# Unread bf16 products streamed through TensorE at four places of a two-layer audio tower

## The chip, the cores and the metric

The kernel runs on one core of a Trainium2 chip. The metric is the device time of one launch in microseconds (us), smaller is better. The core's engines work side by side and meet at semaphores: TensorE (PE, matrix products and transposes into the eight PSUM banks), VectorE (DVE), ScalarE (ACT), GpSimd (POOL, no access to PSUM) and SyncE (SP, which only issues DMAs here). The hardware profiler also records which clock was granted to TensorE: 1.00 in a row is 2.4 GHz, 0.50 is 1.2 GHz.

## What is computed

Sixteen signals of 4096 samples become 16 x 255 tokens of 64 values, and two layers follow, each attention plus a mixture of experts. Cut to what matters:

```python
h = tok(x)                      # interpolate 4x, windows of 64, |fft|, soft minimum: (16, 255, 64)
h = h + attn0(layernorm(h))     # 8 heads, rank 32 scores, softmax over 255 tokens, 64x64 value-output matrix per head
h = h + moe0(layernorm(h))      # 16 experts 64 -> 128 -> 64, relu, top 2; plus own residual and layernorm with gain
h = h + attn1(layernorm(h))     # 8 heads of 8, softmax of content scores blended with a softmax of positions
h = h + moe1(layernorm(h))      # 8 experts 64 -> 64 -> 64, gelu, top 2
```

Everything is fp32 (a few operands are split into bf16 parts that add up to fp32 precision).

## The kernel before

Tokens lie in SBUF as 32 tiles of 128 rows x 64 values (`res`), two tiles per signal; a chunk is 4 tiles, so there are 8 chunks (`CH`, `TC`). The program has two phases with a barrier between them. The phase `tokens` makes the tokens and ends on DVE and ACT, with nothing for PE after its last transform. The phase `experts0_to_experts1` holds both layers as two blocks, `attention0_and_experts0` and `attention1_and_experts1`. In each block every engine has one program, written out by hand with loops over pairs of signals in the middle of the attentions; the order of work on an engine is the order of the text, and semaphores say when a step may start. Engines run from one stage straight into the next, and the stretches where one stage drains and the next fills are called joins here.

**Start of attention 0.** DVE makes averages, variances and the first normed tiles. PE's `x_columns(c)` transposes chunk c into bank 5 or 6 (L695, four 128x128 transposes), ACT or DVE copies it out, POOL makes the normed tiles of chunks 2 to 7 (L1328). `project` makes queries and keys (L708) or values (L712) into banks 7 and 4, ACT copies them (L930), `scores` (L720) writes banks 0 to 3, and DVE takes the maxima (L1152). DVE's `inverse_roots(1, ...)`, for which POOL's L1328 waits, stands behind the first maxima in DVE's order.

**Attention 0 to experts 0.** After the last signal PE runs `outputs_turn` and `weights(0)` (L630, transposes of the routing weights of chunk 0, which DVE makes: L1055, L1057), then `duos`: per chunk and pair of experts `hidden` (L644), ReLU on ACT (L904), `second` (L655), weighting on DVE (L1138, L1097).

**First join, experts 0 to attention 1.** PE turns the positional weights of the eight heads (`pos_turn`, L1671, banks 2 and 3, copied out by ACT in `pos_out`, L1952), turns the chunks of the new input (`x_columns` of this block, that is `ColumnParts.turn`, L404, banks 0, 1, 5), and turns the last sum of the experts (`e0.sum_turn`, L663). ACT, DVE and POOL split each turned chunk into bf16 parts (L409, L413, L419, L420, L424), the last chunks only after the last normalisation of the experts (DVE L1078 to L1089, POOL L465 to L469, ACT L880 and L886). `values(c)` (L1684) and `pos_values(n)` (L1700) use the parts and the turned weights; after that the attention loop starts.

**Second join, attention 1 to experts 1.** `x_turn` (L1784), `logits` (L1797), and the tail of the attention (`slot` with "tail": L1651, L1591, L1597) alternate on PE, while DVE reads the logits and picks experts (`best`, L2215 to L2222), and makes the routing weights of the first four chunks (`combine(0)`, L2233 to L2252). PE's `weights(0)` and `weights(1)` (L1803) wait for these. Then per chunk c and group g: `hidden` (L1817), gelu on ACT (L2048), `spread` (L1829, routing weights to all rows, banks 4 and 5), `weigh` on DVE (L2269), `second` (L1839, L1842), and per chunk `sum_turn` (L1852), with `x_turn` and `logits` of chunks 6 and 7 among the first two chunks. `w64`, which the change reads, holds bf16 weights, written in the phase `tokens` and only read afterwards.

Of the kernel before, what the change touches and what calls it, by code (L numbers as in the profile page):

```python
# [25 lines left out]
P = 128  # L26
B, SIG = 16, 4096
# [16 lines left out]
H = 8  # L44
# [43 lines left out]
def tower(nc, x, taps, consts, w_raw, gate_b0, w1_01, b1_0, w2_0, b2_0, gamma,  # L88
          split_sel, wpos, wproj, bproj, b1_1, w2_1, b2_1, out):
    with ExitStack() as ctx:  # L90
# [4 lines left out]
        ps = ctx.enter_context(nc.psum_tensor("ps", [P, 8, 512], F32))  # L95
# [12 lines left out]
        w64 = sb("w64", [P, 3, W64 - W32], BF16)  # L108
# [43 lines left out]
        def sem(name):  # L152
            held.append(nc.alloc_semaphore(name))
            return held[-1]
# [8 lines left out]

        def chain(eng, name):
            return Chain(eng, sem(name))

# [323 lines left out]
        def attention0_and_experts0(block, later):  # L492
            QUADS = 2
# [45 lines left out]
            def columns_copied(eng, c):  # L539
                if c < BY_ACT:  # L540
                    eng.wait_ge(s_col_a, c + 1)
                else:
                    eng.wait_ge(s_col_d, c - BY_ACT + 1)
# [59 lines left out]
            def _(pe):  # L603
# [83 lines left out]
                def x_columns(c):  # L687
                    if c < 2:
                        pe.wait_ge(s_x, c + 1)
                    else:  # L690
                        pe.wait_ge(s_xp, c - 1)
                    if c >= 2:
                        columns_copied(pe, c - 2)
                    for k in range(TC):
                        last = nc.tensor.transpose(ps[:, COLUMN_BANK[c % 2], P * k:P * k + P], x2[:, TC * c + k].rearrange("p a d -> p (a d)"), ident)  # L695
                    last.then_inc(s_turned, 1)
# [18 lines left out]
                def scores(k):  # L715
                    par, g = at(k)
                    for tq in range(2):
                        for i in range(4):
                            r = slice(32 * i, 32 * i + 32)
                            last = nc.tensor.matmul(S[:, i, tq], qk[par][r, g, 0, P * tq:P * tq + P], qk[par][r, g, 1], start=True, stop=True)  # L720
                    last.then_inc(s_S, 1)
# [22 lines left out]
                def outputs_turn(par):  # L744
                    for tq in range(2):
                        last = nc.tensor.matmul(OT[:, tq], o_sb[par][:, P * tq:P * tq + P], fold[:], start=True, stop=True)
                    last.then_inc(s_OT, 1)
# [18 lines left out]
                def slot(j, k, more=True, route=None):  # L766
# [41 lines left out]
                        route()  # L808
                    second_turn(k, N, 1)

                x_columns(0)
                x_columns(1)
                columns_copied(pe, 0)
                project(QKN, 0, 0, 0)
                pe.wait_ge(s_out, 2)
                scores(0)
                project(VN, 0, 1, 0)
                x_columns(2)
                x_columns(3)
# [20 lines left out]
                pe.wait_ge(s_O, B)  # L840
                pe.wait_ge(s_add, B - 1)
                outputs_turn((B - 1) % 2)
                weights(0)

                duos(0, 0)
# [601 lines left out]
        def attention1_and_experts1(block, e0):  # L1447
            scale = (D // H) ** -0.5
            QUADS = 2
# [97 lines left out]
            def _(pe):  # L1547
# [163 lines left out]
                pos_turn(1)  # L1711
                x_columns(1)
                pos_turn(2)
                x_columns(2)
                pos_turn(3)
                e0.sum_turn()
                for h in range(4, H):
                    pos_turn(h)
                x_columns(3)
                x_columns(4)  # L1720
                values(0)
                x_columns(5)
                values(1)
                x_columns(6)
                values(2)
                x_columns(7)
                values(3)
                project(0, 0)
                pos_values(0)
                pos_values(1)  # L1730
                values(4)
# [130 lines left out]
                x_turn(3)  # L1862
                logits(2)
                x_turn(4)
                slot(B // 2, 6, ("tail",))
                logits(3)
                x_turn(5)
                slot(B // 2, 7, ("tail",))
                logits(4)
                logits(5)  # L1870
                hidden(0, 0)
                pe.wait_ge(s_O, QUADS * B)
                for d in range(2):
                    weights(d)
                for c in range(CH):
                    hidden(c, 1)
                    if c == 0:
                        pe.wait_ge(s_fin, B)
                        for d in range(2, 4):
                            weights(d)  # L1880
                    spread(c, 0)
                    if c >= 1:
                        second(c - 1, 1)
                    if c < 2:
                        x_turn(6 + c)
                    if c == 3:
                        pe.wait_ge(s_wgt, GROUPS * c + 1)
                        for d in range(4, CH):
                            weights(d)
                    if c < CH - 1:  # L1890
                        hidden(c + 1, 0)
                    if c < 2:
                        logits(6 + c)
                    spread(c, 1)
                    if c >= 1:
                        sum_turn(c - 1)
                    if c == 0:
                        pe.wait_ge(s_ct, 4)
                    second(c, 0)
# [626 lines left out]
```

## Time and profile before

| | us |
|---|---|
| median of 3 runs | 752.44 (750.17 to 752.70) |
| profiled execution | 751.62 |
| span of its trace | 749.8 |
| PE busy | 649.9 (87%) |
| DVE busy | 570.5 (76%) |
| ACT busy | 503.1 (67%) |
| POOL busy | 334.4 (45%) |
| mean granted TensorE clock | 0.937 |

The busy times overlap. The end of a matmul is modelled and matmuls are pipelined, so a busy PE isn't PE at its peak. The chain that ended last is 55% PE, 23% DVE and 8% issue by share of the span. In the chain each piece is what the end of the execution waited for at that moment; a piece of PE there can be shorter than the same work in the timeline, since the next piece starts before its modelled end. The clock of 0.937 is an average over long stretches at 1.00 and some at 0.50.

### The profile page before, as it was taken

The numbers are of one execution on the slowest core, as the hardware profiler recorded it, in microseconds if no ns is written. First come the engines' busy times: TensorE is split into PE (matmuls) and PEld (weight loads), VectorE is DVE, ScalarE is ACT, GpSimd is POOL, SyncE is SP. The second block draws the span as 40 slices with busy tenths as digits, with TensorE's granted clock in tenths as the row PEclk, the third lists the DMA queues.
The fourth block names the chain that finished last, engine by engine and source line by source line (L and its number), as shares of the span: only waits on it lengthen the run. The fifth ranks groups of instructions, "written<-read, shape, count | busy, mean of one in ns | idle before, by whom it ended". The sixth has DMA issues, their size and how long they took to land.

```text
span 749.8 us, 16418 instructions
## 1 busy us (share of the span) xinstructions
PE 649.9 (87%) x4984; PEld 357.5 (48%) x4984; DVE 570.5 (76%) x1647; ACT 503.1 (67%) x1264; POOL 334.4 (45%) x417
## 2 busy tenths in 40 slices
PE   5528998999999988999999996799898888779896
PEld 5514665666666653333232225455555555453332
DVE  6675787777777776899999978589888888773653
ACT  3646877888888863567777767477777777624542
POOL 1006678788787866133333325624554545300000
PEclk9857999999999999999999998799999999965998
DMA  4030000000000002523323330000000000000001
GB/s 109 1 112 1 1 2 1 0 0 0 0 0 0 1 1 85 200 102 108 104 98 96 99 109 1 2 2 1 1 0 0 0 0 0 2 0 2 15 19 24
DMA packets 22038, 24.37 MB, mean 33 GB/s; under 512 B 12390, under 2 KB 12902, under 8 KB 21734
## 3 DMA queue, kind: packets, MB, share of 16 engines
q1 hardware_dynamic: 19751, 23.31, 9.9%
q10 hardware_dynamic: 2239, 0.49, 0.3%
q8 instruction: 22, 0.36, 0.2%
q14 instruction: 26, 0.21, 0.1%
HBM read 22.48 MB, written 1.31 MB: 32 GB/s over the span
## 4 chain that ended last, share of the span: by engine, by line
PE 55%; DVE 23%; issue 8%; ACT 3%; POOL 2%; DMA 2%; DVEq 0%; SPq 0%; ACTq 0%; POOLq 0%
PE ps L726 8%; PE ps L762 7%; PE ps L1563 5%; DVE big L1097 4%; PE ps L1585 4%; PE ps L720 4%; DVE big L1138 3%; DVE big L2077 3%; PE ps L1839 2%; PE ps L1569 2%; PE ps L1817 2%; PE ps L644 2%; PE ps L708 2%; PE ps L712 2%; DVE big L1055 2%
## 5 line engine op out<-in xcount | busy, mean ns | idle before, releaser
L1344 POOL TENSOR_TENSOR big<-big 128x1024 f32<-128x1024 f32 x64 | 119.8, 1893 | 45.7 <-DVE big L1158 45.7
L942 ACT ACTIVATE big<-ps,big 128x255 f32<-128x255 f32 x256 | 117.0, 483 | 12.2 <-DVE big L1152 9.7
L904 ACT ACTIVATE big<-ps,b1s 128x512 f32<-128x512 f32 x128 | 80.2, 678 | 32.5 <-PE ps L644 31.1
L1152 DVE TENSOR_REDUCE big<-ps 128x4 f32<-128x1020 f32 x64 | 75.1, 1212 | 26.7 <-PE ps L720 26.7
L1935 ACT ACTIVATE big<-ps 128x1024 f32<-128x1024 f32 x64 | 65.9, 1030 | 33.0 <-PE ps L1575 30.6
L2077 DVE TENSOR_REDUCE big<-ps 128x4 f32<-128x1020 f32 x64 | 78.0, 1219 | 6.9 <-DVE res L2134 2.5
L726 PE MATMUL ps<-cst,big 128*128 128x128 f32 x512 | 76.7, 283 | 6.3 <-POOL big L1344 2.4
L1164 DVE COPY mid<-ps 128x512 f32<-128x512 f32 x96 | 63.4, 685 | 18.3 <-PE ps L726 15.1
L726 PEld LDWEIGHTS ps<-cst,big 128*128 128x128 f32 x512 | 54.2, 140 | 40.8 <-issue 21.5
L644 PE MATMUL ps<-big,wall 64*128 64x512 f32 x256 | 72.8, 645 | 0.7 <-ACT big L875 0.7
L655 PE MATMUL ps<-big,w2s 128*64 128x512 f32 x256 | 69.9, 625 | 2.1 <-ACT big L904 1.2
L762 PE MATMUL ps<-mid,big 128*64 128x256 f32 (+1 forms) x512 | 69.5, 392 | 0.0
L1138 DVE SCALAR_TENSOR_TENSOR big<-ps,b2s,mid 128x512 f32<-128x512 f32 x64 | 47.9, 749 | 18.6 <-issue 8.8
L942 ACT ACTIVATION_READ_ACCUMULATOR big<-ps,big 128x1 f32 x256 | 55.6, 217 | 0.0
L465 POOL TENSOR_TENSOR big<-big 128x4 f32<-128x4 f32 x16 | 16.2, 1015 | 86.1 <-DVE big L455 85.6
L1563 PE MATMUL ps<-big,selqk 128*128 128x256 bf16 x384 | 52.8, 273 | 0.7 <-ACT big L1911 0.4
L1097 DVE TENSOR_TENSOR big<-big 128x512 f32<-128x512 f32 x56 | 44.2, 790 | 0.0
L930 ACT ACTIVATE big<-ps 128x512 f32<-128x512 f32 x64 | 34.9, 600 | 10.8 <-PE ps L708 9.8
L460 POOL TENSOR_TENSOR mid<-mid 128x2 f32<-128x2 f32 x16 | 11.5, 717 | 66.4 <-DVE mid L455 66.4
L1563 PEld LDWEIGHTS ps<-big,selqk 128*128 128x128 bf16 x384 | 32.7, 97 | 17.2 <-issue 13.5
L1569 PE MATMUL ps<-big 64*128 64x256 bf16 x256 | 25.4, 273 | 17.8 <-DVE big L2077 17.6
L720 PE MATMUL ps<-big 32*128 32x256 f32 x512 | 37.6, 408 | 2.9 <-ACT big L942 1.7
(274 smaller groups left out, 1327.9 us busy)
## 6 DMA issues: line engine op xcount, KB each, us to landing
mid<-spread_w SPq DMA_DIRECT2D x128, 128.0 KB, 2.8
mid<-in_split_sel SPq DMA_DIRECT2D x1, 1536.0 KB, 7.4
wall<-in_w SPq DMA_DIRECT2D x1, 1280.0 KB, 6.4
out_tokens<-res SPq DMA_DIRECT2D x16, 56.0 KB, 1.6
cst<-in_consts SPq DMA_DIRECT2D x1, 520.5 KB, 5.0
pexp<-in_w_raw SPq DMA_DIRECT2D x1, 512.0 KB, 6.3
w2s<-in_w SPq DMA_DIRECT2D x1, 512.0 KB, 3.3
mid<-in_taps ACTq DMA_DIRECT2D x1, 320.0 KB, 3.9
```

Source lines behind the costliest of these rows:

```text
L644: last = nc.tensor.matmul(H1(e, j), wst[0][half, f:f + P], xc[q][half], start=True, stop=True)
L655: last = nc.tensor.matmul(Y(e)[D * j:D * j + D], w2s[0][:, 2 * e + j], hid[e % 2][j], start=True, stop=True)
L726: last = nc.tensor.transpose(AT[:, j, c, P * tq:P * tq + P], e_sb[r % 4][:, j, tq, P * c:P * c + P], ident)
L762: last = nc.tensor.matmul(O[D * j:D * j + D, par], val[par][0:n, c, D * h:D * h + D], a_sb[r % 4][0:n, j, c], start=(g == 0 and a == 0 and ...
L904: last = nc.scalar.activation(hid[e % 2][j], H1(e, j), ACT.Relu, bias=b1s[0][:, 2 * e + j:2 * e + j + 1])
L942: last = nc.scalar.activation(e_sb[r % 4][:, jj, tq, 0:NW], S[:, 2 * (r % 2) + jj, tq, 0:NW], ACT.Exp, scale=-1.0, bias=minus[r % 4][:, jj ...
L1097: ins = nc.vector.tensor_tensor(acc[q], acc[q], part[e % 2], ALU.add)
L1138: nc.vector.scalar_tensor_tensor(out=acc[q] if e == 0 else part[e % 2], in0=Y(e), scalar=b2s[:, e:e + 1], in1=cb[e % RING], op0=ALU.add, o ...
L1152: nc.vector.tensor_reduce(minus[r % 4], S[:, 2 * a:2 * a + 2, :, 0:NW], AX.X, ALU.min).then_inc(s_mx, 1)
L1344: nc.gpsimd.tensor_tensor(e_sb[r % 4], e_sb[r % 4], bc(inverse[r % 4].unsqueeze(3), [P, 2, 2, 256]), ALU.mult).then_inc(s_A, 1)
L1563: last = nc.tensor.matmul(out_, selqk[:, 2 * p + n, part], parts[par][:, part], start=(part == 0), stop=(part == 2))
L2077: nc.vector.tensor_reduce(mx[k % 2], S[:, :, :, 0:NW], AX.X, ALU.max).then_inc(s_max, 1)
```

## The change

A helper `stream(bank, n)` issues n products of 128x128 by 128x512 in bf16 from `w64` into one PSUM bank; nothing waits for them, nothing reads them, and what they leave in the bank is overwritten by the next real product. It is called ahead of and among the first columns of attention 0 (14, 2, 3, 5 and 3 products), ahead of the first routing weights of experts 0 (5), in the first join (6, 3, 6, 2, 4, 3 and 6) and in the second (6, 6, 9 and 3): 86 products. Where a bank is still being read, the wait that the next user of the bank has anyway is repeated or moved ahead of the stream. No other instruction changes.

```diff
--- before.py
+++ after.py
@@ -163,6 +163,12 @@
 
         def chain(eng, name):
             return Chain(eng, sem(name))
+
+        def stream(bank, n):
+
+            weights = w64[:].rearrange("p n f -> p (n f)")
+            for _ in range(n):
+                nc.tensor.matmul(ps[:, bank], weights[:, 0:P], weights[:, 0:512], start=True, stop=True)
 
 
 
@@ -808,12 +814,17 @@
                         route()
                     second_turn(k, N, 1)
 
+                stream(0, 14)
                 x_columns(0)
+                stream(0, 2)
                 x_columns(1)
+                stream(0, 3)
                 columns_copied(pe, 0)
                 project(QKN, 0, 0, 0)
+                stream(0, 5)
                 pe.wait_ge(s_out, 2)
                 scores(0)
+                stream(4, 3)
                 project(VN, 0, 1, 0)
                 x_columns(2)
                 x_columns(3)
@@ -840,6 +851,9 @@
                 pe.wait_ge(s_O, B)
                 pe.wait_ge(s_add, B - 1)
                 outputs_turn((B - 1) % 2)
+                pe.wait_ge(s_at, 6 * B)
+                pe.wait_ge(s_at0, 2 * B)
+                stream(4, 5)
                 weights(0)
 
                 duos(0, 0)
@@ -1711,21 +1725,29 @@
                 pos_turn(1)
                 x_columns(1)
                 pos_turn(2)
+                stream(6, 6)
                 x_columns(2)
                 pos_turn(3)
+                stream(6, 3)
                 e0.sum_turn()
                 for h in range(4, H):
                     pos_turn(h)
                 x_columns(3)
                 x_columns(4)
+                stream(6, 6)
                 values(0)
                 x_columns(5)
+                stream(6, 2)
                 values(1)
                 x_columns(6)
+                stream(6, 4)
                 values(2)
                 x_columns(7)
+                stream(6, 3)
                 values(3)
                 project(0, 0)
+                pe.wait_ge(s_ptc, H)
+                stream(3, 6)
                 pos_values(0)
                 pos_values(1)
                 values(4)
@@ -1862,14 +1884,17 @@
                 x_turn(3)
                 logits(2)
                 x_turn(4)
+                pe.wait_ge(s_O, QUADS * B)
+                stream(4, 6)
                 slot(B // 2, 6, ("tail",))
                 logits(3)
                 x_turn(5)
                 slot(B // 2, 7, ("tail",))
+                stream(4, 6)
                 logits(4)
                 logits(5)
                 hidden(0, 0)
-                pe.wait_ge(s_O, QUADS * B)
+                stream(4, 9)
                 for d in range(2):
                     weights(d)
                 for c in range(CH):
@@ -1878,6 +1903,8 @@
                         pe.wait_ge(s_fin, B)
                         for d in range(2, 4):
                             weights(d)
+                        pe.wait_ge(s_lc, 5)
+                        stream(5, 3)
                     spread(c, 0)
                     if c >= 1:
                         second(c - 1, 1)
```

## Rows read from the trace of the kernel before

**Rows 1.** windows: length, busy us of PE, PEld, DVE, ACT, POOL, then granted clock

```profile
50.60:65.50 14.90, 13.01 (x56) 7.81 (x56) 9.33 (x19) 10.21 (x28) 6.76 (x8) 0.50 0.16 64
458.10:461.40 3.30, 3.30 (x18) 2.92 (x17) 2.90 (x22) 1.94 (x4) 1.19 (x2) 0.50 0.00 0
461.60:464.60 3.00, 0.99 (x9) 0.71 (x7) 2.29 (x5) 2.82 (x7) 2.65 (x5) 1.00 0.03 5
464.70:475.00 10.30, 6.57 (x63) 4.68 (x63) 8.80 (x28) 8.68 (x18) 8.04 (x10) 0.51 0.00 2
656.00:662.60 6.60, 5.75 (x59) 4.48 (x51) 3.93 (x34) 2.73 (x6) 0.59 (x1) 1.00 0.00 1
662.90:674.20 11.30, 7.74 (x43) 5.44 (x43) 9.12 (x66) 1.75 (x5) 0.89 (x2) 0.50 0.00 0
678.40:693.40 15.00, 15.00 (x41) 6.11 (x42) 5.58 (x21) 5.01 (x10) 0.00 (x0) 0.50 0.00 1
707.30:710.70 3.40, 3.40 (x15) 1.25 (x14) 1.69 (x3) 0.60 (x1) 0.00 (x0) 0.51 0.12 24
```

**Rows 2.** chain that ended last, start of attention 0: start us, us, engine, line

```profile
65.71 1.07 PE ps L720 x16
...
68.10 1.14 DVE big L1152
```

**Rows 3.** timeline, same stretch: start us, us, what, [idle before <-releaser]

```profile
50.64 1.97 PE L695 MATMUL ps<-cst,big 128*128 128x128 f32 x8 [21.62 <-DVE big L1223]
...
55.80 2.09 PE L720 MATMUL ps<-big 32*128 32x256 f32 x16 [1.19 <-ACT big L930]
...
56.05 0.06 DVE L443 MEMSET big<- 128x2 f32 x1
...
59.47 6.03 POOL L1328 TENSOR_TENSOR big<-mid,rowsc 128x512 f32<-128x512 f32 x6 [6.29 <-DVE rowsc L1219]
```

**Rows 4.** chain, first join

```profile
458.24 3.46 PE ps L1671 x16
...
462.35 1.43 ACT big L880 x4
...
475.09 3.64 PE ps L1700 x16
...
485.44 1.95 PE ps L1700 x16
```

**Rows 5.** timeline of POOL, first join

```profile
461.49 0.20 POOL L469 TENSOR_TENSOR big<-big 128x4 f32<-128x4 f32 x1
```

**Rows 6.** waits of PE, 450 to 480 us: total us, times, longest

```profile
PE ps L1684 <- POOL cols_area L424: 3.9, 4, 2.0
```

**Rows 7.** timeline of PE, ahead of the first experts

```profile
288.01 0.60 PE L630 MATMUL ps<-cst,big 128*16 128x128 f32 x4 [1.78 <-DVE big L1057]
```

**Rows 8.** chain, second join

```profile
672.12 0.56 DVE mid L2252
...
677.37 0.96 PE ps L1829 x2
...
679.38 2.01 PE ps L1817 x4
...
697.49 1.06 PE ps L1817 x4
698.55 0.53 PE ps L1829 x2
699.08 1.03 PE ps L1839 x4
```

**Rows 9.** timeline, second join

```profile
663.13 0.47 PE L1651 MATMUL ps<-cst,big 128*128 128x128 f32 x1 [1.15 <-POOL big L2335]
...
676.31 1.26 ACT L2048 ACTIVATE big<-ps,b1s 128x512 f32<-128x512 f32 x2
...
696.36 1.28 DVE L2269 TENSOR_TENSOR big<-big,ps 128x512 f32<-128x512 f32 x2
```

## Prediction

> **What bounds the kernel now.** I read the windows first, for the clock that was granted to TensorE (PE), then the chain of waits through the stretches where it is low, then the timeline there for what PE waits on. [Rows 1]: the windows at 0.50 are the start of attention 0 (13.01 us busy of 14.9 from 50.6), most of the join of experts 0 to attention 1 (458.1 to 461.4, and from 464.7 until L1700's 3.64 us are through, at 478.7 [rows 4]), and the join of attention 1 to experts 1, from 662.9 to 693.4 without a break. 0.50 is the 1.2 GHz level, 1.00 the 2.4 GHz one. The last stretch is the dear one: from 678.4 to 693.4 PE is busy in all 15.00 us, so it is the bound, at half speed. One more low stretch (707.3 to 710.7) lies where the change puts nothing. Elsewhere the change can move little.
>
> What PE did before each turn of the clock: it rose to 1.00 after a stretch in which PE was busy throughout at 0.50 (3.30 of 3.30 us up to 461.4, then 1.00; L1700's 3.64 us before 478.7), and fell after a sparse one (0.99 of 3.00 us from 461.6, then 0.51) [rows 1, 4]. But busy time alone doesn't hold it: it fell after 5.75 of 6.60 us busy up to 662.6, where much of the work is 8-column routing products and 128-column transposes, and stayed low through the 15 busy us after 678.4, where half of the products use only 64 or 24 rows. A stream of 128-row, 512-column bf16 products is denser than any of these, so I expect it both to lift and to hold the clock.
>
> **Price of one streamed product.** None is in the trace. The nearest is L1829, 512 columns in bf16 over 24 rows: two take 0.96 us in the chain at half clock and 0.53 at full [rows 8], so 0.48 and 0.27 each; these are upper values. The Trainium skill ("TensorE: Matmul & The Clock Gate", Back-to-back issue gap) has N/1.2 ns and N/2.4 + 2.5 ns, 0.43 and 0.22 us here; by it the sum below would be some 0.3 us better, as fewer streams overrun their wait.
>
> **Start of attention 0 (14, 2, 3, 5 and 3 products).** PE idles 21.62 us before its first L695 at 50.64 [rows 3]; the phase itself begins at about 44.4, after the barrier. Fourteen products at 0.48 are 6.7 us, with a clock that rises on the way about 5.5: they end before or just about where the first transposes can start, cost nothing (at most 0.5 if the clock never rises), and leave the clock up. Then the chain is: four transposes (eight take 1.97, so 1.0, and 0.5 at full clock), ACT copy, L708, two ACT copies L930, L720 with 2.09 from 55.80, and DVE's L1152 right behind it [rows 3]. L720 at full clock is 1.07 [rows 2]; L708, as long as L720 at half clock, shares its ratio: about 1.05. I laid this out anew: transposes from 50.64 to 51.2, L708 51.9 to 53.0 (3 products, 0.8, end with the copy that it waits for), L930 53.6 to 54.75 (ACT has two other instructions ahead of it; 5 products, 1.35, end at 54.4 beside them), L720 to 55.9. L1152 could start at 55.9, but DVE is busy with what stands before it to 56.1 [rows 3]: 1.8 to 1.9 us earlier. Behind it POOL's six L1328 start at 57.6 for 59.47 [rows 3]. PE's half-rate L695 and L708 after 60.57 are on the chain too, so the next L1152 (68.10, [rows 2]) comes 2.3 earlier by the same laying out; POOL's unbroken row of work allows no more. **2.3 us**, bounds 1.9 (POOL's shift) and 2.9 (all PE pieces at full clock).
>
> **Ahead of the first experts (5 products).** They are put ahead of L630, which waits 1.78 us for DVE's L1057 [rows 7]. Five are 1.35 us: hidden. The two waits in front (turned blocks copied) are for copies that ended some 4 us before. The clock is 1.00 there already, so nothing is gained: **0**, bounds -0.3 and +0.3.
>
> **First join (30 products).** The DVE chain up to L663 doesn't change; the streams of 6 (1.6 us) and 3 (0.8) lie in PE's waits for DVE's L1138 and L1097, over 2 us and about 0.8. Sixteen transposes L1671 take 3.46 us at half clock [rows 4]. At full clock they are paced by ACT's copy (0.60 each), so the last copy ends about 1 us earlier; but ACT's next, L880 at 462.35, also needs POOL's L469, ended at 461.69 [rows 4, 5]. So 0.55. From there to 475 the chain runs over ACT, POOL and DVE; PE's half-rate pieces lie beside it, as do the streams of 6, 2, 4 and 3 (each 0.5 to 1.6 us, ahead of L1684, which waits 3.9 us for POOL in four times [rows 6]). The last six, 1.6 us from about 472.8, end at 474.5, when L1700 can start 0.55 early. L1700 is 3.64 at half clock and 1.95 at full, both x16 [rows 4]: 1.7. **2.2 us**, bounds 0 (clock falls again between the streams, and the last six, 2.9 us at half clock, delay L1700 while they lift the clock for it) and 2.4.
>
> **Second join (24 products).** (a) Six ahead of L1651, where PE idles 1.15 us [rows 9]: 6 x 0.27 = 1.6, a delay of 0.5, against L1651 and eight L1797 at full clock, 0.5 less: 0. (b) Six, later nine, up to L1803, which follows DVE's L2252, which ends at 672.7 [rows 8]: DVE's chain is unbroken from 664.7 to there, and with the clock up PE is through the nine (2.4 us) at about 671. Nothing is gained or lost, but PE then idles over 1 us, where the clock could fall. (c) Hidden, transposes, three products (0.8) and L1829 at full clock: then the first weighing (DVE L2269) is bound by ACT's gelu, which ends at 677.57 [rows 9], instead of starting at 678.44: 0.85. (d) Then, with full-clock prices [rows 8]: weigh 1.28, normalise 0.6, routing (L2215 to L2222) 1.4 after a wait of 0.5 for its logits, weigh 1.3: 682.6. Then PE: L1829 0.53, L1839 1.03, L1784 0.6, L1817 1.06, L1797 0.64: 686.5. Then DVE: routing and difference 1.65: the fourth weighing starts at 688.1. Before it starts at 696.36 [rows 9]. So (c) and (d) together are 8.2. As a check: 15.00 us of PE-bound work [rows 1] at L1817's ratio of 1.06 to 2.01 [rows 8] would shrink by 7.1; (d) has 7.35. Behind it the order of work is the same at the same clock. I take **7.5**, near the full layout, because hand-overs tend to eat some tenths; bounds 5.2 (clock falls once in the idle time of (b) and comes back about 680) and 8.2.
>
> **Sum.** 2.3 + 0 + 2.2 + 7.5 = 12.0. The profiled execution took 751.62 us (span 749.8); 751.62 - 12.0 = 739.6. It lies 0.8 under the median of the runs, 752.44, to which I hold the forecast: **740.4 us**.
>
> **Rivals.** (1) *One join isn't held.* The clock falls in a wait that no stream covers (PE still idles about 1.5 us around L1803; between L1684s) and part of the half-rate stretch returns. For: the clock fell after 0.99 us busy of 3.00 [rows 1]. Against: each gap left is shorter than that. Gain 7.1 (1.9 + 0 + 5.2): 745, from 743 to 748. (2) *The streams lift nothing and cost nothing*: unread products don't count as work, but all lie in waits: 752. Against: nothing in the rows tells read from unread. (3) *Slower.* The clock is at 1.2 GHz when a stream begins and stays there, so that each product is 0.48. Place: the nine ahead of L1803 most of all: with the six before them PE's half-rate work, which ended at 670.8, ends 1.9 later, then 4.3 of stream: L1803 starts at 677.0 for 672.8, 4.2 late, and three more add 1.4. At the start PE runs 0.5 + 2.6 + 1.3 = 4.4 late, in the first join 0.7 + 1.2. Together +11.9: 764. It decides if a stream of 6 us leaves the clock at 0.50; the rises after 3.3 and 3.6 busy us [rows 1, 4] speak against it. (4) *Transposes don't count as activity.* Then both joins, full of transposes, would fall between streams and only the start and the expert products would gain: 2.3 + 0 + 5.2: 745. Against: from 458.1 to 461.4 PE did almost nothing but L1671 transposes, and the clock went from 0.50 to 1.00 [rows 1, 4].
>
> The Trainium skill (same page, PE-mode transpose) says that the clock's full rate doesn't engage for transposes. By that rule rival (4) holds; this trace speaks against it.
>
> **How the numbers follow.** Forecast 0.60; rival (1) 0.27; (2) 0.05; (3) 0.05; (4) 0.03. The range goes from 735.5 (all upper bounds, 2.9 + 0.3 + 2.4 + 8.2, and the stretch after 707.3 and one like it gone too, about 1.4 each as estimated from 3.4 us at half clock in part hidden: 735.8) to 747.0 (rival (1) and most of its spread). About 0.5% (3.8 us) is what a measurement of this kernel can tell from no change: faster is the forecast, (4) and nearly all of (1), 0.89; within it (2) and the rest of (1), 0.06; slower 0.05.
>
> **What would show it.** Right: PEclk at 1.00 from about 50 us on and through both joins; L708 at 1.1; DVE's L2269 pairs in the second join 3 us apart on average instead of 6; the gap from L2252 to the fourth weighing 15.5 us for 23.7. Wrong: 0.50 in the second join after the nine products; L1651, L1803 or L1700 waiting for a stream; a new low stretch elsewhere, in a loop, that takes back what is gained.

## The result, and the profile after

The changed kernel takes 739.03 us (median, 737.55 to 743.12); the kernel before, beside it, 751.77 (750.17 to 752.70). The ratio is 0.985, 95% interval 0.9805 to 0.9895, which excludes 1: faster, 12.7 us by the medians for the 12.0 of the sum (11.3 by the ratio, 7.9 to 14.7). A ratio leaves out executions more than 1.5% above the fastest of their kernel, so it can differ from the ratio of two medians. The forecast was 740.4 (735.5 to 747.0). The profiled execution took 737.55 us.

The page of the changed kernel: span, busy times, granted clock in 40 slices.

```profile
span 735.8 us, 16590 instructions
...
PE 645.7 (88%) x5070; PEld 353.0 (48%) x5070; DVE 570.9 (78%) x1647; ACT 502.1 (68%) x1264; POOL 334.1 (45%) x417
...
PEclk9869999999999999999999999999999999999998
```

PE, DVE, ACT and POOL are each busy within 5 us of what they were, although PE has 86 products more. The mean clock rose from 0.937 to 0.983. Line numbers moved: L695, L708, L720, L1152 and L1328 are now L701, L714, L726, L1166 and L1342; L663 and L1700 are L669 and L1714; L1803, L1817, L1829, L1839 are L1825, L1839, L1851, L1861; L2252 and L2269 are L2279 and L2296. The streams are L171.

Windows of the changed kernel over the same stages as [rows 1] (length, busy us of PE, PEld, DVE, ACT, POOL, then the granted clock):

```profile
44.70:49.00 4.30, 4.24 (x11) 1.52 (x12) 3.69 (x6) 2.11 (x3) 0.00 (x0) 0.50 0.55 169
49.00:65.10 16.10, 13.62 (x98) 7.58 (x96) 12.18 (x26) 10.51 (x29) 8.22 (x8) 1.00 0.26 87
449.20:471.30 22.10, 16.00 (x137) 9.99 (x135) 19.82 (x63) 18.04 (x38) 12.94 (x20) 1.00 0.01 2
...
656.00:666.70 10.70, 8.77 (x60) 4.74 (x60) 9.01 (x60) 1.47 (x4) 1.16 (x2) 1.00 0.01 2
666.80:682.70 15.90, 14.52 (x86) 7.37 (x88) 10.49 (x71) 10.97 (x18) 0.70 (x1) 1.00 0.01 2
694.00:697.50 3.50, 3.50 (x20) 1.84 (x20) 1.34 (x3) 1.32 (x3) 0.00 (x0) 0.52 0.18 37
```

The 0.50 level is left only from 32 to 49.0, that is in PE's idle time ahead of the first fourteen products and under most of them, at 694 to 697.5, and from 731.7 to the end, where PE has nothing to do. The start of attention 0 from its first transposes on and both joins run at 1.00 throughout.

The timeline of the changed kernel, PE unless another engine is named (start us, us, what, [idle before <-releaser]):

```profile
44.76 5.27 PE L171 MATMUL ps<-w 128*128 128x512 bf16 x14 [15.46 <-PEq L162]
50.93 0.66 PE L701 MATMUL ps<-cst,big 128*128 128x128 f32 x4 [0.90 <-DVE big L1237]
...
54.10 1.25 PE L171 MATMUL ps<-w 128*128 128x512 bf16 x5
55.35 1.15 PE L726 MATMUL ps<-big 32*128 32x256 f32 x16
...
58.08 2.04 POOL L1342 TENSOR_TENSOR big<-mid,rowsc 128x512 f32<-128x512 f32 x2 [4.60 <-DVE rowsc L1233]
59.17 0.66 PE L701 MATMUL ps<-cst,big 128*128 128x128 f32 x4 [0.86 <-POOL big L1342]
...
60.99 1.13 PE L714 MATMUL ps<-big,pexp 64*128 64x256 f32 x8 [0.17 <-ACT big L944]
...
65.10 1.21 DVE L1166 TENSOR_REDUCE big<-ps 128x4 f32<-128x1020 f32 x1
...
469.11 1.46 PE L171 MATMUL ps<-w 128*128 128x512 bf16 x6
471.29 1.95 PE L1714 MATMUL ps<-pos_t,vall 128*64 128x256 f32 x16 [0.72 <-DVE vall L2168]
...
663.05 2.12 PE L171 MATMUL ps<-w 128*128 128x512 bf16 x9
666.79 0.65 PE L1825 MATMUL ps<-ident_b,mid 128*96 128x128 bf16 x8 [1.62 <-DVE mid L2279]
668.33 1.13 PE L1839 MATMUL ps<-big,wall 64*128 64x512 f32 x4 [0.89 <-DVE mid L2242]
...
671.67 1.28 DVE L2296 TENSOR_TENSOR big<-big,ps 128x512 f32<-128x512 f32 x2 [1.12 <-PE ps L1851]
...
682.70 1.28 DVE L2296 TENSOR_TENSOR big<-big,ps 128x512 f32<-128x512 f32 x2
...
693.92 1.80 PE L1861 MATMUL ps<-big,w2s 128*64 128x512 f32 x4
695.65 1.94 PE L1825 MATMUL ps<-ident_b,mid 128*96 128x128 bf16 x16
```

To be seen here: PE waits 0.90, 0.72 and 1.62 us behind the fourteen, the last six and the nine, so none of these delays what follows. L1714 takes 1.95 for the 3.64 of [rows 4], L714 1.13. A product costs 1.46 / 6 = 0.24 us, or 2.12 / 9, at full clock. The weighings run from 671.67 to 682.70, where before the first came at 678.44 and the fourth at 696.36 [rows 9]. The last two rows are half-clock ones (four L1861 take 1.08 at 677.53). This low stretch isn't new: it begins 11.4 us behind the fourth weighing, under the same work as the one at 707.3 in [rows 1], which begins 10.9 us behind it.

To say where the time went I cut the program at seven instructions of the timeline. The **start** runs from the first DMA issue of the phase (44.44 before) to the third set of maxima (68.02). **Experts 0** runs from the first L630 to the L663 of the last sum, the **first join** from there to the first values behind L1700's 16 products. **Weights** is from `x_turn(0)` to the end of L2252, and **second join** from there to the fourth weighing. The other stages are attention 0 (219.9 to 221.1 us, but 222.8 in join1_only), attention 1 (177.7 to 179.8) and what follows the fourth weighing (52.4 to 54.3). All numbers are us of one profiled execution each, but for the median and range, which are those of all executions.

| kernel | median (range) | span | start | experts 0 | first join | weights | second join |
|---|---|---|---|---|---|---|---|
| before | 751.77 (750.17-752.70) | 749.8 | 23.58 | 169.14 | 21.51 | 16.32 | 23.68 |
| after | 739.03 (737.55-743.12) | 735.8 | 20.38 | 168.72 | 19.43 | 15.78 | 15.97 |
| start_only | 749.28 (743.54-755.91) | 746.1 | 20.38 | 172.10 | 22.15 | 15.79 | 18.48 |
| join1_only | 746.84 (737.85-754.24) | 752.4 | 22.00 | 172.59 | 19.45 | 15.80 | 23.28 |
| join2_only | 746.80 (741.71-750.96) | 744.3 | 23.49 | 169.94 | 22.80 | 15.79 | 17.21 |
| thin | 751.57 (746.03-759.45) | 747.2 | 23.70 | 172.19 | 23.14 | 16.07 | 16.45 |
| all_again | 738.71 (736.42-742.70) | 734.6 | 20.38 | 167.73 | 19.43 | 15.81 | 15.98 |
| transposes | 739.27 (736.31-740.62) | 738.8 | 20.38 | 171.54 | 19.46 | 15.81 | 15.99 |
| filled_both | 738.63 (737.77-740.41) | 738.6 | 20.38 | 171.98 | 19.43 | 15.80 | 15.98 |
| no_nine | 739.36 (one) | 737.6 | 20.39 | 168.63 | 19.45 | 15.80 | 17.56 |
| before_again | 754.46 (one) | 752.7 | 22.45 | 172.63 | 23.25 | 15.80 | 22.98 |
| before_third | 754.59 (one) | 752.8 | 22.57 | 170.23 | 22.07 | 16.32 | 23.70 |
| doubled | 748.14 (742.81-749.12) | 744.7 | 23.87 | 171.71 | 19.88 | 16.99 | 16.63 |
| chunks_filled | 743.50 (741.14-745.92) | 742.5 | 20.38 | 172.72 | 19.43 | 15.79 | 17.18 |

### The profile page after: what moved, and what is told of

The parts are those of the page before. It is cut to its first block and busy times, and to the rows that moved or that the text cites. A ratio compares the mean times of both kernels' runs of the same rounds, so it can differ in the third digit from the quotient of the medians.

```text
span 735.8 us, 16590 instructions
## 1 busy us (share of the span) xinstructions
PE 645.7 (88%) x5070; PEld 353.0 (48%) x5070; DVE 570.9 (78%) x1647; ACT 502.1 (68%) x1264; POOL 334.1 (45%) x417
## 5 line engine op out<-in xcount | busy, mean ns | idle before, releaser
L1166 DVE TENSOR_REDUCE big<-ps 128x4 f32<-128x1020 f32 x64 | 75.1, 1212 | 25.0 <-PE ps L726 25.0
L1152 DVE SCALAR_TENSOR_TENSOR big<-ps,b2s,mid 128x512 f32<-128x512 f32 x64 | 47.8, 749 | 18.1 <-DMA mid<-spread_w 8.7
L1111 DVE TENSOR_TENSOR big<-big 128x512 f32<-128x512 f32 x56 | 44.1, 787 | 0.0
L1577 PEld LDWEIGHTS ps<-big,selqk 128*128 128x128 bf16 x384 | 32.7, 97 | 17.2 <-issue 13.5
L1583 PE MATMUL ps<-big 64*128 64x256 bf16 x256 | 25.4, 273 | 17.8 <-DVE big L2104 17.6
L768 PEld LDWEIGHTS ps<-mid,big 128*64 128x64 f32 (+1 forms) x512 | 31.1, 136 | 18.8 <-issue 7.9
```

Source lines behind the costliest of these rows:

```text
L768: last = nc.tensor.matmul(O[D * j:D * j + D, par], val[par][0:n, c, D * h:D * h + D], a_sb[r % 4][0:n, j, c], start=(g == 0 and a == 0 and ...
L1166: nc.vector.tensor_reduce(minus[r % 4], S[:, 2 * a:2 * a + 2, :, 0:NW], AX.X, ALU.min).then_inc(s_mx, 1)
L1577: last = nc.tensor.matmul(out_, selqk[:, 2 * p + n, part], parts[par][:, part], start=(part == 0), stop=(part == 2))
```

## Experiments: one place at a time

My theory was the prediction's: the streams gain by the clock alone, and the three places add up. The rival was that one place brings the clock up for the others, or that moved waits and not the clock make the gain.

**start_only**, **join1_only** and **join2_only** keep the streams of one place and take the others out, moved waits included. For start_only, against the changed kernel:

```diff
-                stream(4, 5)
...
-                stream(6, 6)
...
-                pe.wait_ge(s_O, QUADS * B)
-                stream(4, 6)
...
-                stream(4, 9)
```

> Only the five streams at the start of attention 0 (27 products) are kept. Theory (each place gains by its own clock, and the gains add): the granted clock is 1.00 from about 49 us on, the second block of maxima of attention 0 comes about 3.0 us earlier as in the changed kernel, both joins stay at 0.50 as before; time 751.8 - 3.1 = 748.7, from 747.7 to 749.8. Rival (the start gains only what the first POOL work moves, 1.9 us, and the rest of the 3 us seen was chance): 749.9. Rival (the clock once up stays up through the joins, by whatever it was lifted): 740.

Measured: 0.9962 of before (0.992 to 1.0005), 749.28 us for 750.40. Its start is 20.38, the same as with all streams, and its first join stays at 22.15. But its second join, where it has no stream, took 18.48 in place of 23.68. The median lies in the expected range, but the interval doesn't exclude that nothing was gained.

> Only the seven streams of the first join (30 products) are kept. Theory: clock 1.00 through that join, L1700 at 1.95 us, 2.1 us gained between the last sum of experts 0 and the end of L1700, nothing elsewhere: 751.8 - 2.1 = 749.7, from 748.5 to 750.8. Rival (the streams hold the clock only where it comes in high from the start): no gain, 751.8.

Measured: ratio 0.9921 (0.9877 to 0.9965), 746.84 us. First join 19.45, second 23.28. The median is below the expected range (748.5 to 750.8), though the first join gained the 2.1 that was expected; why the median gained more, these runs don't show. The profile is of its longest execution, 754.24, with a start of 22.00 and a further low stretch at 118 to 121.5.

> Only the four streams of the second join (24 products) are kept. Theory: clock 1.00 from 656 to the fourth weighing, 8.2 us gained from there, 0.6 in the routing before it if the six products ahead of L1651 don't delay it: 751.8 - 8.5 = 743.3, from 742 to 745.5. Rival (the clock falls in the unfilled idle time around L1803, and comes back some us later): 5.2 gained, 746.6.

Measured: ratio 0.9933 (0.9895 to 0.9971), 746.80 us. The median is above the expected range (742 to 745.5), at the 746.6 of the expectation's rival, and a fall around L1803 did come. Second join 17.21 and not 15.97 (windows of join2_only):

```profile
656.00:676.00 20.00, 15.90 (x137) 10.12 (x137) 14.79 (x109) 5.83 (x14) 2.34 (x4) 1.00 0.01 1
676.50:680.50 4.00, 4.00 (x17) 1.38 (x15) 1.80 (x17) 3.51 (x5) 0.70 (x1) 0.57 0.00 0
```

The clock fell once, right behind PE's idle time around `weights(0)`, and was back within 4 us. That costs 1.2 us, where the rival counted on 3.

What follows from the profiles, one of each kernel: each place does its own part, 20.38 at the start, 19.45 in the first join and 17.2 in the second, whatever stands at the others. The times show it less cleanly, since each kernel that leaves a place unfilled spreads over 9 to 16 us. By the ratios and 750.40 us the three gains are 2.9, 5.9 and 5.0 us, together 13.8, about the whole; by the plain medians they are 1.1, 3.6 and 3.6, together 8.3; by the plain means of all executions 1.6, 4.4 and 5.0, together 11.0. The intervals (-0.4 to 6.0, 2.6 to 9.2, 2.2 to 7.9) allow both, so the share of each place in the median isn't settled by these runs.

## Experiments: what the products do

**thin** keeps every stream, wait and weight load, and shortens each product to 16 columns:

```diff
-                nc.tensor.matmul(ps[:, bank], weights[:, 0:P], weights[:, 0:512], start=True, stop=True)
+                nc.tensor.matmul(ps[:, bank, 0:16], weights[:, 0:P], weights[:, 0:16], start=True, stop=True)
```

> All 86 products are there, at the same places and behind the same waits, but with 16 columns instead of 512: as many instructions and weight loads, almost no columns streamed. Theory (it is the density of the streamed columns that lifts and holds the clock): the clock is low in the same stretches as in the kernel before, mean near 0.937, 751.8 within 1.5. Rival (what gains is that PE is issued to without a pause, or the moved waits): clock near 0.98, 739. Rival (weight loads count half): only the longest streams lift the clock, 745.

Measured: 1.002 of before (0.9975 to 1.0066). Windows of thin:

```profile
49.00:65.00 16.00, 13.24 (x68) 8.34 (x69) 10.24 (x21) 10.04 (x28) 6.38 (x7) 0.50 0.21 81
667.00:683.00 16.00, 12.12 (x89) 8.38 (x88) 12.88 (x97) 5.15 (x10) 1.85 (x3) 0.58 0.00 1
```

and its timeline:

```profile
44.17 0.52 PE L171 MATMUL ps<-w 128*128 128x16 bf16 x14 [15.46 <-PEq L162]
50.33 1.11 PE L701 MATMUL ps<-cst,big 128*128 128x128 f32 x4 [5.63 <-DVE big L1237]
```

Fourteen thin products are over in 0.52 us, PE idles 5.63, and the first transposes run at half clock (1.11 for 0.66). The start took 23.70 and the first join 23.14. So at these two places, and in the whole time, the moved waits and the mere issue of instructions gain nothing; the gain needs products that work through the wait. The second join of thin was short all the same (16.45), so for that place thin settles nothing; it is taken up below.

**transposes** streams two fp32 transposes of 128x128 in place of each product. It tests rival (4).

```diff
-                nc.tensor.matmul(ps[:, bank], weights[:, 0:P], weights[:, 0:512], start=True, stop=True)
+                for k in range(2):
+                    nc.tensor.transpose(ps[:, bank, P * k:P * k + P], ident, ident)
```

> Each of the 86 products of 512 columns in bf16 is replaced by two fp32 transposes of 128x128 (identity by identity) into the same bank, at the same places. In the kernel before, eight such transposes take 1.09 us at full clock, so a pair takes about 0.27, as the product it replaces. Theory from the profile (L1671's transposes alone lifted the clock at 461.4): clock up as in the changed kernel, 739 to 742. Rival (transposes don't count as activity, which is what the Trainium skill says of them): as before, 751, or slower by the overruns at half clock.

Measured: 739.27 us beside 738.71 of **all_again**, which is the changed kernel once more on the same chip; the ratios to before are 0.9827 (0.9743 to 0.991) and 0.985 (0.9762 to 0.9937). Timeline of transposes:

```profile
44.59 4.84 PE L172 MATMUL ps<-cst 128*128 128x128 f32 x28 [15.47 <-PEq L162]
50.76 0.66 PE L702 MATMUL ps<-cst,big 128*128 128x128 f32 x4 [1.33 <-DVE big L1238]
```

and its windows:

```profile
44.70:49.00 4.30, 4.30 (x26) 4.30 (x27) 3.86 (x6) 1.97 (x3) 0.00 (x0) 0.63 0.64 178
49.00:65.00 16.00, 13.08 (x110) 9.16 (x108) 12.08 (x27) 10.52 (x29) 8.27 (x8) 1.00 0.24 85
```

With nothing but transposes before it the clock rose to 1.00 ahead of the real work, and the four stages last what they last with products (20.38, 19.46, 15.81, 15.99). The Trainium skill ("TensorE: Matmul & The Clock Gate", PE-mode transpose) says that the full rate doesn't engage for transposes. Both this run and [rows 1, 4] speak against it.

> The changed kernel once more, beside the kernel before on one chip, as the mark for the other kernels of this group. Theory (the four groups of streams lift and hold the clock in every execution): median 739, no time over 745, mean clock at least 0.975 in each. Rival (its 739 was luck with where the clock turned, as the times of the kernel before spread from 745 to 760): median 743 or more and a spread of over 8 us.

Measured: 738.71 us (736.42 to 742.70), at mean clocks of 0.978 to 0.987, as the theory said.

**no_nine** takes out only the nine products ahead of `weights(0)`.

```diff
-                stream(4, 9)
```

> The changed kernel without the nine products between hidden(0, 0) and the routing weights of experts 1. Theory (PE would then stand nearly idle for some 4 us there): the clock falls about when the routing weights are ready, and the stretch from them to the fourth weighing grows from 16.0 us to between 17 and 22. Rival (the six products before it and hidden suffice): 16.0 us.

Measured: 739.36 us, second join 17.56 for 15.98. Timeline of no_nine:

```profile
667.64 1.09 PE L1825 MATMUL ps<-ident_b,mid 128*96 128x128 bf16 x8 [3.68 <-DVE mid L2278]
669.18 2.08 PE L1839 MATMUL ps<-big,wall 64*128 64x512 f32 x4 [0.46 <-DVE mid L2241]
```

PE idles 3.68 us, comes back at half clock (1.09 for 0.65, 2.08 for 1.13) and is at 1.00 again from 673.3. Of the 7.7 us between the second joins of before and after, 1.6 hang on the nine.

**filled_both** asks for more: six more products ahead of `weights(0)`, and nine at chunk 3, where the low stretch at 694 began. There no bank is free, so these multiply by zero weights and add nothing to a sum under way.

```diff
+                nc.tensor.matmul(ps[:, bank], xab[:, 0, B, 0:P], weights[:, 0:512], start=False, stop=False)
...
-                stream(4, 9)
+                stream(4, 15)
...
+                    if c == 3:
+                        add_nothing(6, 4)
...
+                    if c == 3:
+                        add_nothing(6, 5)
```

> The changed kernel plus: 15 products instead of 9 ahead of the routing weights of experts 1 (PE still waited 1.62 us there), and nine bf16 products of a zero block, added into the open sum in bank 6, around hidden(3, 1) in the routing stall of chunk 3 (PE waited 0.95 and 1.04 us there, and the clock fell at 694). Theory (the last low stretch costs L1839's bank 1.80 for 1.03 us and L1825 1.94 for about 1.0): clock 1.00 to the end, 1.6 us less than the changed kernel, 737.4. Rival (a zero block doesn't count as activity): clock still falls there and nothing is gained, 739. Rival (the six more products overrun the wait): 740.

Measured: 738.63 us, no different from 738.71. Timeline of filled_both:

```profile
312.61 1.08 PE L675 MATMUL ps<-fold,big 128*128 128x64 f32 x8 [1.63 <-DVE big L1047]
313.62 2.03 PE L656 MATMUL ps<-big,wall 64*128 64x512 f32 x4
...
695.43 1.25 PE L171 MATMUL ps<-w,cols_area 128*128 128x512 bf16 x5
...
697.14 1.08 PE L1867 MATMUL ps<-big,w2s 128*64 128x512 f32 x4
```

The low stretch at 694 is gone (L1867 1.08, where L1861 of the changed kernel took 1.80), in this one profile. The last engine work ends 47.4 us behind the fourth weighing, for 48.0 in the two profiles of the changed kernel, so the stretch was worth 0.6, under half of the 1.6 expected. Only 0.3 of it reaches the end, since what follows that work took 5.4 for 5.1. no_nine, join2_only and thin had neither that stretch nor the nine products of chunk 3, and their work ended at 47.3. In exchange this execution has low stretches in experts 0, at 313.5 and 436.5 (the first is in the rows: L656 2.03 for 1.13), which neither profile of the changed kernel has.

## Experiments: how steady the kernel before is

start_only and thin had a shorter second join without dense streams in it. So I profiled the kernel before twice more, changed in a comment only (**before_again**, **before_third**).

> The kernel before, once more, unchanged but for a comment. Theory A (the clock's turns in the kernel before differ from one execution to the next): its low stretches in the joins don't lie where they lay in the first profile; the time from the routing weights of the first four chunks (end of L2252) to the fourth weighing, 23.7 us there, comes anywhere between 16 and 24, and the whole time follows the mean granted clock, some 745 at 0.955 and 760 at 0.928. Theory B (the stretch before the fourth weighing is always low): 23.7 within 0.5, and the low stretch from 662 to 694 is there again within 1 us.

> The same kernel as before_again with another comment. Theory A: its two joins differ from those of before_again and of the first profile, by up to 7 us in the second. Theory B: all three profiles show the same stretches.

Measured: the second join took 22.98 and 23.70, which is theory B's size; the start took 22.45 and 22.57 for 23.58, the first join 23.25 and 22.07 for 21.51. Windows of before_again:

```profile
51.50:58.50 7.00, 5.30 (x34) 2.93 (x32) 5.97 (x15) 4.91 (x9) 0.73 (x1) 0.79 0.19 80
...
62.00:65.50 3.50, 3.50 (x28) 2.18 (x24) 0.78 (x2) 2.12 (x8) 3.50 (x4) 0.62 0.02 5
...
671.00:695.50 24.50, 22.10 (x78) 9.84 (x79) 13.48 (x71) 8.05 (x13) 1.40 (x2) 0.50 0.00 1
```

At the start the clock rose once, fell again and rose, where in [rows 1] it stayed down to 65.5. The low stretch of the second join is there in all three profiles, but it begins at 662.9 in one and later in the others (668.8 and 665.9). before_third has one more at 287 to 297. Neither theory holds alone: the first two places change from one execution to the next, while the second join is low each time. In the kernel before, then, the same code takes 741.8 to 759.9 us over all executions measured beside these kernels. Two of them show what goes with it: 745.25 at a mean clock of 0.955, 759.86 at 0.928. Both are from one group of 35 executions on one chip, so it isn't the chip that makes the difference.

## Experiments: the price of a product too many

**doubled** issues each stream twice as long.

```diff
-                stream(0, 14)
+                stream(0, 28)
...
-                stream(4, 9)
+                stream(4, 18)
```

> Every stream has twice its products, 172 for 86. It prices a product that doesn't fit into its wait. Theory A (a product is 0.22 us at full clock, and what overruns a wait is paid in full): in the profile of the changed kernel PE waits 0.90 us behind the fourteen, 0.63 behind the five, 1.18, 0.81, 0.52, 0.74, 0.58 and 0.72 behind streams of the first join and 0.39 and 1.62 in the second; the rest overruns. Start: 28 products end 3.0 later, 2.1 over, and the others add 2.4 at most: 2.1 to 4.5. Experts: 0.5. First join: 1.3, mostly at the six ahead of the sum's turn and the last six, 0.5 to 2. Second join: 1.3 and 0.9 lie ahead of DVE's choosing of experts, 0.4 and 0.65 behind: 1 to 3.3. Sum 4.1 to 10.3: about 746 for 738.7, between 743 and 749. Theory B (the waits have room that the hidden ends of matmuls don't show): under 742. Theory C (double streams cost more than that, as a stream delays DVE and ACT work that comes back to PE): over 750, slower than or like the kernel before.

Measured: 748.14 us (742.81 to 749.12), as theory A said; 0.9973 of before (0.993 to 1.0016). Timeline of doubled:

```profile
45.03 7.46 PE L171 MATMUL ps<-w 128*128 128x512 bf16 x27 [15.86 <-PEq L162]
52.33 0.60 PE L701 MATMUL ps<-cst,big 128*128 128x128 f32 x4
...
672.54 3.83 PE L171 MATMUL ps<-w 128*128 128x512 bf16 x17 [0.16 <-issue]
676.21 0.61 PE L1825 MATMUL ps<-ident_b,mid 128*96 128x128 bf16 x8
```

No wait is left ahead of L701 and L1825: the streams set when they start. Against the changed kernel the start is 3.5 longer, the first join 0.45, the weights 1.2, the second join 0.7; experts 0, which ends behind nine extra products, 3.0, but low stretches at 317.5 and 440 are in that too. So the waits had little room, and most of the gain can be spent by 86 products more.

**chunks_filled** tried to stop the falls in experts 0. PE waits there once in a chunk ahead of the sum's turn, and I put four products into that wait:

```diff
-                    pe.wait_ge(s_acc, c + 1)
                     if not last_chunk:
                         pe.wait_ge(s_lc, c + 3)
+                        stream(7, 4)
...
+                    pe.wait_ge(s_acc, c + 1)
```

> The changed kernel with four more products ahead of each sum turn of experts 0 but the last (L669, into bank 7, once its last reader is through). PE waits there once in a chunk for DVE's L1041, 1.44 to 1.63 us, and behind just this gap the clock fell in some of the profiles (313.5 to 318 and 436.5 to 440.5 in two of the variants of the changed kernel, with L650 at 2.03 and 2.08 for 1.13 us behind it), in others not. Four products are 1.0 us: they fit. Theory A (the gap is what lets the clock fall): no low stretch from 286 to 453; the stretch from the first routing weights to the last sum turn takes 167.7, as in the one profile without any, where others took up to 172; the median is 736.5, between 735 and 738, and the runs lie closer together. Theory B (the falls in the loops come from something else): they are there again, median 738.7. Theory C (the products delay the sum or the next chunk): over 739.5.

Measured: 743.50 us (741.14 to 745.92), 4.8 more than the changed kernel: theory C. Waits of PE in chunks_filled, from 286 to 455 (total us, times, longest), and its timeline:

```profile
PE ps L171 <- DVE big L1045: 7.0, 6, 1.5
...
PE ps L673 <- DVE big L1115: 0.5, 1, 0.5
```

```profile
313.56 0.81 PE L171 MATMUL ps<-w 128*128 128x512 bf16 x3 [1.49 <-DVE big L1045]
314.21 1.00 PE L673 MATMUL ps<-fold,big 128*128 128x64 f32 x8
```

The same waits in the changed kernel:

```profile
PE ps L669 <- DVE big L1041: 6.5, 6, 1.6
PE ps L669 <- DVE big L1111: 1.4, 1, 1.4
```

I had misread the first row. DVE's L1041 (L1045 here) reads the logits out of bank 7: it is not the sum that PE waits for, but the bank itself, and the stream writes that bank. So the products of six sets stand behind the wait and not in it, and each is paid: 313.56 to 314.21 is 0.65 us, six of them are 3.9, and experts 0 took 172.72 for 168.72 and 167.73. The seventh set, ahead of the last sum turn but one, lies in a wait for L1111 (1.4 us, 0.5 behind the products) and costs nothing. This profile also has low stretches at 69 to 72.4 and at 673 to 676.5, with 1.2 us each in attention 0 (221.1 for 219.9) and the second join, where no product was put in. Theory A has this much for it, that there is no low stretch between 72.5 and 671; with one profile, and two of the changed kernel that had none in experts 0 either, that settles nothing. A bank that nobody guards there would be needed, and that wasn't tried.

## Point by point

- **The bound.** Right. The low stretches at the start and in the two joins held the gain: of the 14.0 us between the two spans, 3.2, 2.1 and 8.2 lie there (the last with the 0.5 ahead of the routing weights), together 13.5. Against before_again and before_third the terms shift, 2.1, 3.8 and 7.0 in the one and 2.2, 2.6 and 7.7 in the other, without the 0.5; their sums, 12.9 and 12.5, stay near the 13.0 of the first profile. One more low stretch of the kernel before isn't in the prediction, in experts 0:

```profile
437.40:441.10 3.70, 3.70 (x10) 0.80 (x8) 1.27 (x6) 2.24 (x6) 0.00 (x0) 0.54 0.45 134
```

  It wasn't there in the two profiles of the changed kernel, which has no product near it, and came back in four of its variants; experts 0 was 0.4 and 1.4 us shorter.
- **Price of a product.** 0.24 and less, under the 0.27 taken as an upper value. The formula of the Trainium skill ("TensorE: Matmul & The Clock Gate", Back-to-back issue gap) gives 0.22. Nine in 2.12 us agree to 0.02. The fourteen took 5.27 with the rise on the way; 5.5 was laid out.
- **Start: predicted 2.3, measured 3.2, above the upper bound of 2.9.** This is the mis-sized term. The first part was nearly right: POOL's L1342 starts 1.67 earlier, counted from the start of the phase, for 1.87 laid out. The step that failed is "POOL's unbroken row of work allows no more". Once POOL's first tile is there, what the third maxima wait for is mostly PE's chain. In the kernel before (timeline) PE had

```profile
60.57 2.11 PE L695 MATMUL ps<-cst,big 128*128 128x128 f32 x8 [0.66 <-POOL big L1328]
62.61 2.08 PE L708 MATMUL ps<-big,pexp 64*128 64x256 f32 x8
```

  both at half clock; from this first L695 to the maxima were 7.45 us (60.57 to 68.02) and in the changed kernel 5.93 (59.17 to 65.10). That is 1.5 us where I had left 0.4. But two other profiles of the kernel before had a start of 22.45 and 22.57, since the clock was partly up there, and against these the gain is 2.1 and 2.2: the term depends on which execution of the kernel before one holds it to. And the start isn't safe behind its end: start_only, no_nine and chunks_filled, three of the eight profiles with these streams, fell again at 69 to 72.5 and spent 221.1 us on attention 0 for 219.9.
- **First experts: 0.** L636 still waits 0.63 us behind the five products. Attention 0 has the same length in both, 219.99 and 219.93.
- **First join: predicted 2.2, measured 2.1.** L1714 gained 1.69 of the 1.7. The streams are hidden, with a wait behind the last six. Against the other two profiles it is 3.8 and 2.6.
- **Second join: predicted 7.5 of a full layout of 8.2; measured 7.7 for the same parts, (c) and (d), and 8.2 with (a), by that profile.** The parts: (a) was to be 0 and brought 0.5, the time from `x_turn(0)` to the routing weights, 16.32 to 15.78; but before_again has 15.80 without streams, so this is not theirs. (c) From the routing weights to the first weighing 5.76 became 4.94, so 0.82 for 0.85. (d) From the first to the fourth weighing 17.92 became 11.03, so 6.9 for 7.35. The gap that I named, 23.7 to 15.5, became 15.97. Hand-overs did eat some tenths. The weighings are 3.7 us apart on average for 6.0; the 3 of the prediction didn't follow from its own layout, which gives 3.5.
- **A fall around L1803.** I had it as possible, at 2.3 us (5.2 for 7.5). It came in join2_only and chunks_filled and cost 1.2 each. The size was wrong by half, because the clock comes back within 4 us there.
- **Rivals.** (1) didn't come in the changed kernel's two profiles (there 15.97 and 15.98), and came once in a variant with all its streams (chunks_filled), where it cost 1.2 in the join, and not the 4.9 between forecast and rival. (2) and (4) are refuted by the result and by transposes. (3) needs a stream that leaves the clock low; it rose after 4.3 us. doubled shows the mechanism of its price, overrun, at 9.4 us against all_again.
- **What I missed.** The kernel before is not one time, and 740.4 was held to a median that itself came out between 750.4 and 753.5 in the groups: that the forecast hit to 1.4 us is in part luck. The spread of 742 to 760 (74 executions) narrows to 736 to 743 (8 executions). With it goes that the start and both joins, where the clock used to turn at a place that changed, now last the same to 0.03 us in four of the five profiles that have every wait filled (after, all_again, transposes, filled_both; chunks_filled fell once, in the second join). What is left to vary is experts 0, 167.73 to 171.98 with low stretches of 3 to 4 us in some executions, attention 0 with the fall at 69, and the stretch at 694, which costs 0.6 and is the one of 707.3 in the kernel before, not a new one.

Open: why the second join of start_only and thin was 18.48 and 16.45 with no dense stream in it, when the three profiles of the kernel before and join1_only have 23.0 to 23.7. In both the clock came back at 683 instead of 694 to 697 under the same work. I have no run that says why. So a short second join doesn't prove the streams at work: all eight profiles with dense streams there have 16.0 to 17.6, but so has one of the six without. That the dense products bring the gain as a whole rests on the times, 736 to 743 for the changed kernel and 746 to 759 for thin.

## To carry to other kernels

Where PE waits and a low clock follows, on the path that sets the end, products that nobody reads buy that stretch back at 0.22 to 0.24 us each, as long as they fit: count PE's idle time behind each stream in the profile afterwards, and take out what shows none. Put them ahead of the wait and into a bank that isn't guarded by the same semaphore; read first which of several waits came last. Profile the kernel before more than once: what seems a fixed cost of a stage can be one draw of where the clock turned.

## What the chip showed

- The clock's turns lie elsewhere in each execution of the same program: 741.8 to 759.9 us for identical code. In the three profiles of the kernel before the clock first rose in the second phase at 65.5, 54.4 and 54.9 us, with the phase beginning within 0.2 us of the same time. The Trainium skill ("TensorE: Matmul & The Clock Gate", What's actually happening) says that the transition point varies by about 0.5 us either way, with where the first matmul lands. The profiles agree that it varies, but by 11 us.
- PE can be busy in every microsecond and stay at 0.50: 15.00 of 15.00 us in [rows 1], and 22.10 of 24.50 in before_again. In the changed kernel nearly the same work (14.52 of 15.90 us) stays at 1.00 once it enters at 1.00.
- Idle time doesn't decide alone either: 1.62 and 0.89 us around L1825 left the clock at 1.00 in the changed kernel, and nearly the same two waits were followed by a fall in join2_only.
- 28 fp32 transposes lift the clock as 14 bf16 products do, and nine products with zero weights lay among the work around 694 with the clock at 1.00, in one profile.
